# Two whole gathered columns per step fetched row by row, and running maxima stored eight columns at a time, in a three-layer graph network

## The chip, the core and the metric

The kernel runs on one core of one Trainium2 chip. The core has five engines with a queue of instructions each: TensorE (PE), VectorE (DVE), ScalarE (ACT), GpSimd (POOL) and SyncE (SP). Sixteen DMA engines serve them. The metric is the device time of one execution in microseconds (us); less is better.

## What is computed

`x` has 6250 rows (nodes) of 128 features. 200,000 edges `(src, dst)` are sorted by `dst`. After a layer norm and a ReLU, three layers each take, for every node, the maximum over its incoming edges of the source node's row, and add two products:

```python
def _sage_conv(x, src, dst, Wl, bl, Wr):
    agg = jax.ops.segment_max(x[src], dst, num_segments=x.shape[0])
    agg = jnp.where(jnp.isfinite(agg), agg, 0.0)
    return agg @ Wl + bl + x @ Wr

h = jnp.maximum(_layernorm(x, axis=-1), 0.0)
h = leaky_relu(_sage_conv(h, src, dst, Wl1, bl1, Wr1), 0.01)   # 128 -> 256 features
h = leaky_relu(_sage_conv(h, src, dst, Wl2, bl2, Wr2), 0.01)   # 256 -> 256
h = leaky_relu(_sage_conv(h, src, dst, Wl3, bl3, Wr3), 0.01)   # 256 -> 128
return x + h
```

The rows gathered are 128 floats (512 B) wide in layer 1 and 256 floats (1 KB) in layers 2 and 3.

## The kernel before

**Tiling.** The sorted edges are cut into 512 runs of 391 edges. Partition p holds four runs (`CHAINS = 4`), so one *column* is 128 edges, one in each partition, and a *group* is four columns, one edge of each of the 512 runs. Each layer walks 1564 columns in 28 steps: 27 steps of 56 columns (`STEPS - 1`, `RING_COLS`) and a last one of 52. The buffer `ring` in SBUF holds one step: 7 blocks of 8 columns, 14 groups.

**Gathers.** POOL fetches a column with one indirect DMA (L448): 128 rows of the feature table into 128 partitions. Its order of work is a plain loop over blocks and columns. Before block b of the next step it waits until DVE has scanned that block and SP has stored it (`logged[b]`).

**Rows fetched one by one.** 160 rows of every step but the last don't come through POOL: the 128 rows of column 55 and the last 32 of column 54. POOL gathers only 96 rows of column 54. SP issues 72 of these rows, 8 at a time (`fetch_rows` at L1215, nine times a step, each behind a store), and ACT issues 88, 11 at a time (`fetch_rows` at L1140, eight times in a row). Each time the engine first reads 8 or 11 row addresses from the SBUF tile `row_at` into registers (a TENSOR_LOAD, put down to L321, inside `row_places`), then issues one DMA of one row for each (L1231, L1155). A step's rows can be asked for only when block 6 of the step before has been stored (`logged[BLOCKS - 1]`); ACT also waits until DVE has used the first group of its own step (`group_scanned`).

**Scan.** For each group g, DVE adds a restart mask to the running maximum of group g-1 (L758), waits for the data of group g, and takes the maximum in place (L792). At an even g it waits for a block's gathers, at g = 13 (`GROUPS - 1`, columns 52 to 55) for the rows of SP and ACT (L785 to L790). When the first add of block b+1 is through, it stages the indices of block b (L739), which also tells POOL and SP that block b is scanned.

**Log.** SP stores every group to a log in HBM, two stores per block: the first four columns (L1240) when `group_scanned` says so, the last four (L1246) when `block_scanned` does. At the end of a layer the rows that end a node's edges are gathered from this log (L475) and projected.

**ACT's other work.** In the first 25 steps of a layer ACT also moves two tiles through PE for the `x @ Wr` part (`keep_pair`: L1104, L1109, L1118, in layer 1 also L1125 to L1131). It stands in program order behind the step's rows and ahead of the next step's.

Of the kernel before, what the change touches and what calls it, by code (L numbers as in the profile page):

```python
# [11 lines left out]
U32 = mybir.dt.uint32  # L12
U8 = mybir.dt.uint8

P = 128
BLOCKS = 7
# [15 lines left out]
SYNC_ROWS, SYNC_AT_ONCE = 72, 8  # L32
ACT_AT_ONCE = 11
ROWS = 160
# [8 lines left out]
def gnn_program(nc, x, src, dst, weights, out, nodes):  # L43
# [40 lines left out]

    ROWS_OF = [(0, SYNC_ROWS), (SYNC_ROWS, ROWS - SYNC_ROWS)]
    FETCHED = [DMA * count for _, count in ROWS_OF]
    assert LAST <= RING_COLS - CHAINS and all(f * (STEPS - 1) < 1 << 16 for f in FETCHED)
    assert SYNC_ROWS % SYNC_AT_ONCE == 0 and (ROWS - SYNC_ROWS) % ACT_AT_ONCE == 0
    assert SYNC_ROWS // SYNC_AT_ONCE <= GROUPS - 3

    def by_pool(b, last):

        return width(b, last) - (b == BLOCKS - 1 and not last)
# [3 lines left out]
    STORES_OF = [width(b, False) // CHAINS for b in range(BLOCKS)]  # L97
# [7 lines left out]
    with ExitStack() as ctx:  # L105
# [173 lines left out]
        LOADS = 8  # L279
# [29 lines left out]
        def list_of(edges_src):  # L309

            pairs = []
            for first, count, run in ((0, P, (CHAINS - 1) * P), (P, ROWS - P, (CHAINS - 1) * P - (ROWS - P))):
                chain = run * RUN + GROUPS - 1
                pairs.append((row_list[:, first:first + count],
                              bass.AP(edges_src.tensor, chain, [[GROUPS, STEPS - 1], [RUN, count]])))
            return pairs
# [25 lines left out]
        def _(pool):  # L342
# [48 lines left out]
            with pool.If(pool.value_load(unsorted[0:1, 0:1], min_val=0, max_val=1 << 24)):  # L391
# [23 lines left out]
                pool.wait_ge(list_loaded, 2 * DMA)  # L415
                with nc.allow_non_contiguous_dma(reason="one word of each row to fetch"):
                    for here, there in list_of(sorted_src):
                        pool.dma_start(here, there).then_inc(sort_done, DMA)
                pool.wait_ge(sort_done, DMA * (3 + LOADS))

            for l, (w, _n) in enumerate(shapes):
# [12 lines left out]
                def gather(i, first, last):  # L434
                    for b in used_blocks(last):
# [9 lines left out]
                        for u in range(by_pool(b, last)):  # L445
                            c = b * BLOCK_COLS + u
                            rows = 2 * P - ROWS if c == RING_COLS - 2 and not last else P
                            pool.indirect_dma_start(  # L448
                                ring[0:rows, c * w:(c + 1) * w], None, tables[l],
                                bass.IndirectOffsetOnAxis(  # L450
                                    ap=stage[0:rows, b, u:u + 1].bitcast(U32), axis=0),
                            ).then_inc(late_landed if last and b == LATE_BLOCK and u >= CHAINS else landed[b], DMA)
# [29 lines left out]
        def _(dve):  # L482
# [207 lines left out]
            dve.wait_ge(list_loaded, 2 * DMA)  # L690
# [488 lines left out]
        def _(sp):  # L1179
# [27 lines left out]
            with nc.allow_non_contiguous_dma(reason="one word of each row to fetch"):  # L1207
                for here, there in list_of(src):
                    sp.dma_start(here, there).then_inc(list_loaded, DMA)
# [3 lines left out]
            for l, (w, n) in enumerate(shapes):  # L1213

                def fetch_rows(i, g):  # L1215

                    first = g * SYNC_AT_ONCE
# [11 lines left out]
                    places = row_places(0, mybir.EngineType.SP, i, first, SYNC_AT_ONCE, w)  # L1229
# [79 lines left out]
```

## Time and profile before

| what | value |
|---|---|
| median of 3 runs | 6050.79 us (6049.64 to 6051.76) |
| the profiled execution | 6050.56 us |
| its span | 6048.9 us |
| POOL busy | 4524.8 us, 75% |
| DVE busy | 2893.5 us, 48% |
| PE busy | 732.5 us, 12% |
| ACT busy | 225.4 us, 4% |
| DMA busy share | 0.36 in layer 1, 0.68 in layers 2 and 3 |

"Busy" doesn't count the issue of a DMA, register loads or waits, so an engine that only issues DMAs (SP, and ACT in its row fetches) looks idle here. What such an engine does is seen in the timeline and at the sources, where its entries are named SPq and ACTq. Layer 1 runs from 45 to about 1960 us, layer 2 from 2037 to 3962, layer 3 from 4044 to 5969.

### The profile page before, as it was taken

What the parts mean: (1) busy time and instruction counts of PE and PEld (TensorE: products, weight loads), DVE (VectorE), ACT (ScalarE), POOL (GpSimd) and SP (SyncE); (2) the same over time, 40 slices, a digit from 0 to 9 for tenths busy, and PEclk for the clock granted to TensorE, in tenths of its full rate; (3) what the DMA queues carried; (4) which work ended last, traced back from release to release, by engine and by line L of the source; (5) the groups of instructions that cost most, each with busy time, mean ns of one, the idle gap of its engine ahead of it and who ended that gap; (6) DMA issues with size and microseconds to landing.
All of it is one profiled execution on the core that took longest, in us unless ns stands there. A gap on an engine that the chain in (4) does not pass through costs nothing.

```text
span 6048.9 us, 53349 instructions
## 1 busy us (share of the span) xinstructions
PE 732.5 (12%) x2214; PEld 411.8 (7%) x2214; DVE 2893.5 (48%) x3638; ACT 225.4 (4%) x664; POOL 4524.8 (75%) x4793
## 2 busy tenths in 40 slices
PE   1111111111100311111111110040010000100003
PEld 0000000000000200000000000030000000000002
DVE  5333333333333555555555555565555555555556
ACT  1000000000000100000000000010000000000001
POOL 6777777777777777777777777767777777777776
PEclk7555555555555655555555555575555555555556
DMA  4333333333333566666666666666666666666665
GB/s 141 108 111 107 108 108 109 110 108 108 108 108 107 171 216 218 218 216 220 216 218 218 216 219 214 215 206 219 217 220 215 218 218 216 220 215 218 215 216 175
DMA packets 461123, 1089.10 MB, mean 180 GB/s; under 512 B 116295, under 2 KB 181740, under 8 KB 461068
## 3 DMA queue, kind: packets, MB, share of 16 engines
q0 software_dynamic: 203520, 519.10, 30.6%
q1 hardware_dynamic: 220508, 544.04, 24.8%
q10 hardware_dynamic: 37040, 25.45, 1.5%
q14 instruction: 48, 0.39, 0.0%
q8 instruction: 7, 0.11, 0.0%
HBM read 555.08 MB, written 533.07 MB: 180 GB/s over the span
## 4 chain that ended last, share of the span: by engine, by line
POOL 49%; issue 17%; DMA 1%; POOLq 1%; DVE 0%; PE 0%; DVEq 0%
POOL ring L448 47%; POOL ring L475 2%; POOLq L444 0%; DMA ring<-running_max_log,end_row 0%; POOLq L441 0%; DMA patch<-running_max_log,patch_row 0%; DMA ring<-features,stage 0%; DMA running_max_log<-patch 0%; POOL patch L465 0%; DVE z_sum L902 0%; DVE agg L894 0%; POOLq L455 0%; POOLq L443 0%; DMA features<-h_out 0%; DVE patch L873 0%
## 5 line engine op out<-in xcount | busy, mean ns | idle before, releaser
L448 POOL DMA_INDIRECT ring<-features,stage x4611 | 4360.0, 946 | 1432.2 <-issue 1383.7
L792 DVE TENSOR_TENSOR ring<-banks,ring 128x1024 f32<-128x1024 f32 (+1 forms) x1173 | 1227.4, 1046 | 2954.0 <-DMA ring<-features,stage 2918.9
L758 DVE TENSOR_TENSOR banks<-ring,banks 128x1024 f32<-128x1024 f32 (+1 forms) x1173 | 1232.1, 1050 | 37.5
L975 PE MATMUL banks<-wr,h_turned 128*128 128x256 f32 (+1 forms) x490 | 220.7, 596 | 3623.4 <-ACT h_turned L1109 3623.4
L975 PEld LDWEIGHTS banks<-wr,h_turned 128*128 128x128 f32 x490 | 127.2, 320 | 3687.4 <-ACT h_turned L1109 3678.6
L991 PE MATMUL banks<-dst_low,own 128*128 128x394 bf16 x200 | 100.4, 502 | 976.0 <-DVE own L734 976.0
L475 POOL DMA_INDIRECT ring<-running_max_log,end_row x147 | 142.9, 972 | 65.6 <-issue 43.9
L1109 ACT ACTIVATE h_turned<-banks 128x256 f32<-128x256 f32 (+1 forms) x147 | 51.8, 353 | 3128.6 <-issue 2664.1
L739 DVE COPY stage<-edges 128x8 int32 (+1 forms) x588 | 119.4, 203 | 88.0 <-DVE banks L758 32.8
L977 PE MATMUL banks<-b,ones 1*128 1x256 f32 (+1 forms) x294 | 157.6, 637 | 0.0
L1048 PE MATMUL banks<-wl,agg 128*128 128x256 f32 (+1 forms) x490 | 110.7, 369 | 1.2 <-DVE agg L894 0.9
L992 PE MATMUL banks<-dst_high,own 128*128 128x394 bf16 x200 | 99.1, 496 | 0.0
L991 PEld LDWEIGHTS banks<-dst_low,own 128*128 (+1 forms) x200 | 27.8, 139 | 1023.0 <-issue 1021.8
L967 PE MATMUL banks<-ident,h_in 128*128 128x128 f32 x245 | 86.6, 436 | 27.8 <-DMA h_in<-features 27.8
L1125 ACT ACTIVATE signs<-banks,node 128x391 bf16<-128x391 f32 x50 | 29.6, 592 | 1505.5 <-issue 1501.8
L1048 PEld LDWEIGHTS banks<-wl,agg 128*128 128x128 f32 x490 | 84.3, 210 | 11.1 <-DVE agg L894 4.0
L977 PEld LDWEIGHTS banks<-b,ones 1*128 1x128 f32 x294 | 72.9, 307 | 74.4 <-issue 74.4
L1175 ACT ACTIVATE agg<-zeros 128x512 f32<-128x512 f32 x75 | 47.3, 631 | 761.1 <-PE banks L1048 761.1
L1017 PE MATMUL banks<-ident,ring 128*128 128x128 f32 x20 | 5.0, 425 | 577.8 <-DVEq L804 577.8
L1036 PE MATMUL banks<-ident,ring 128*128 128x128 f32 x245 | 59.2, 319 | 62.7 <-DMA ring<-running_max_log,end_row 59.0
L1118 ACT ACTIVATE own<-banks 128x256 f32 (+3 forms) x147 | 51.1, 348 | 394.0 <-PE banks L977 394.0
L883 DVE TENSOR_SCALAR finite<-banks 128x512 int32<-128x512 int32 (+2 forms) x75 | 44.3, 591 | 42.1 <-PE banks L1036 41.2
(114 smaller groups left out, 523.4 us busy)
## 6 DMA issues: line engine op xcount, KB each, us to landing
running_max_log<-ring SPq DMA_DIRECT2D x782, 512.0 KB, 3.1
running_max_log<-ring SPq DMA_DIRECT2D x391, 256.0 KB, 2.2
ring<-features ACTq DMA_DIRECT2D x4752, 1.0 KB
ring<-features,stage POOLq DMA_INDIRECT x4611, 3.2
ring<-features SPq DMA_DIRECT2D x3888, 1.0 KB
ring<-features ACTq DMA_DIRECT2D x2376, 0.5 KB
ring<-features SPq DMA_DIRECT2D x1944, 0.5 KB
h_in<-features ACTq DMA_DIRECT2D x98, 128.0 KB, 2.5
```

The costliest lines, as they stand in the source:

```text
L448: pool.indirect_dma_start(ring[0:rows, c * w:(c + 1) * w], None, tables[l], bass.IndirectOffsetOnAxis(ap=stage[0:rows, b, u:u + 1].bitcast ...
L475: pool.indirect_dma_start(ring[:, t * w:(t + 1) * w], None, logs[w], bass.IndirectOffsetOnAxis(ap=end_row[:, t:t + 1].bitcast(U32), axis=0 ...
L739: dve.tensor_copy(stage[:, b, :], src_t[:, bass.ds((i + ahead) * RING_COLS + b * BLOCK_COLS, BLOCK_COLS)]).then_inc(block_scanned, 1)
L758: dve.tensor_tensor(sum_ps[:, 0:CHAINS * w].rearrange("p (h f) -> p h f", h=CHAINS), group(g - 1).rearrange("p (h f) -> p h f", h=CHAINS), ...
L792: dve.tensor_tensor(group(g), sum_ps[:, 0:CHAINS * w], group(g), ALU.max).then_inc(turn, 1)
L967: turn = pe.transpose(turn_ps[0][:, c * P:(c + 1) * P], h_in[p][:, c * P:(c + 1) * P], ident[:, :])
L975: pe.matmul(mm_ps[p][:, 0:n], h_turned[p][:, c, :], wr_sb[l][:, c, :], start=(c == 0), stop=False)
L977: pe.matmul(mm_ps[p][:, 0:n], ones[0:1, :], b_sb[l][:, :], start=False, stop=True).then_inc(own_mm, 1)
L991: pe.matmul(sel_ps[p][:, 0:RUN + 3], chosen, dst_low[:, h, :], start=(h == 0), stop=False)
L992: mm = pe.matmul(sel_ps[p][:, 0:RUN + 3], chosen, dst_high[:, h, :], start=False, stop=(h == CHAINS - 1))
L1036: turn = pe.transpose(turn_ps[b][:, t * w + c * P:t * w + (c + 1) * P], ring[:, k * w + c * P:k * w + (c + 1) * P], ident[:, :])
L1048: mm = pe.matmul(mm_ps[b][:, t * n:(t + 1) * n], agg[b][:, t * w + c * P:t * w + (c + 1) * P], wl_sb[l][:, c, :], start=(c == 0), stop=(c ...
```

## The change

- Rows fetched one by one are now exactly two columns, 54 and 55 (`FETCHED_COLS = 2`): 256 rows a step. SP fetches the 128 of column 55, ACT the 128 of column 54. POOL issues 54 gathers a step and none of fewer than 128 rows.
- SP reads 16 addresses at a time and issues 16 rows, eight times a step: two such groups behind each of the stores of blocks 0 to 3. ACT reads 32 addresses at a time and issues 32 rows, four times.
- In all steps but the last SP stores a block with one store of eight columns, after the whole block is scanned. The last step keeps its stores of four columns.

```diff
-SYNC_ROWS, SYNC_AT_ONCE = 72, 8
-ACT_AT_ONCE = 11
-ROWS = 160
+FETCHED_COLS = 2
+SYNC_ROWS = 128
+AT_ONCE, ACT_AT_ONCE = 16, 32
...
     def by_pool(b, last):
 
-        return width(b, last) - (b == BLOCKS - 1 and not last)
+        return width(b, last) - (FETCHED_COLS if b == BLOCKS - 1 and not last else 0)
...
-    STORES_OF = [width(b, False) // CHAINS for b in range(BLOCKS)]
+    STORES_OF = [1 for b in range(BLOCKS)]
...
-            before, p = divmod(ROWS_OF[k][0] + r, P)
-            c = RING_COLS - 1 - before
-            p += before * (2 * P - ROWS)
+            ahead, p = divmod(ROWS_OF[k][0] + r, P)
+            c = RING_COLS - 1 - ahead
...
-                            rows = 2 * P - ROWS if c == RING_COLS - 2 and not last else P
                             pool.indirect_dma_start(
-                                ring[0:rows, c * w:(c + 1) * w], None, tables[l],
+                                ring[:, c * w:(c + 1) * w], None, tables[l],
...
-                        if columns > CHAINS:
+                        if last and columns > CHAINS:
                             sp.wait_ge(group_scanned, i * BLOCKS + (FIRSTS * l + b + 1))
                             sp.dma_start(log_block(l, i, b, 0, CHAINS), ring[:, c * w:(c + CHAINS) * w]
                                          ).then_inc(logged[b], DMA)
-                            if not last and BLOCK_GROUPS * b * SYNC_AT_ONCE < SYNC_ROWS:
-                                fetch_rows(i, BLOCK_GROUPS * b)
                         sp.wait_ge(block_scanned, i * BLOCKS + (SIGNED * l + BLOCKS + b + 1))
-                        at = columns - CHAINS
-                        sp.dma_start(log_block(l, i, b, at, CHAINS), ring[:, (c + at) * w:(c + columns) * w]
+                        at = columns - CHAINS if last else 0
+                        sp.dma_start(log_block(l, i, b, at, columns - at), ring[:, (c + at) * w:(c + columns) * w]
                                      ).then_inc(logged[b], DMA)
-                        if not last and (BLOCK_GROUPS * b + 1) * SYNC_AT_ONCE < SYNC_ROWS:
-                            fetch_rows(i, BLOCK_GROUPS * b + 1)
+                        for g in (BLOCK_GROUPS * b, BLOCK_GROUPS * b + 1):
+                            if not last and g * AT_ONCE < SYNC_ROWS:
+                                fetch_rows(i, g)
```

The waits for the loaded lists (`list_loaded`, `LOADS`) follow the number of columns; the two lists are now two columns of `row_list`.

SP, the start of the loop over layer 2's steps, before. ISA and REGISTER_ALU are waits and register work, `ring` 128x1024 is a group of four columns.

```order
L1240 ISA
L1240 DMA running_max_log<-ring 128x1024
L1228 ISA
L321 ISA
L321 TENSOR_LOAD row_at
L1231 DMA ring<-features 1x1024 x8
L1244 REGISTER_ALU
L1246 ISA
L1246 DMA running_max_log<-ring 128x1024
L321 REGISTER_ALU
```

The same place now; `ring` 128x2048 is a block of eight columns.

```order
L1240 ISA
L1240 DMA running_max_log<-ring 128x2048
L1224 ISA
L319 ISA
L319 TENSOR_LOAD row_at
L1227 DMA ring<-features 1x1024 x16
L319 REGISTER_ALU
L319 TENSOR_LOAD row_at
L1227 DMA ring<-features 1x1024 x16
L1238 REGISTER_ALU
```

Between two stores SP now has 32 rows and two loads of 16 registers, where it had 8 rows and one load of 8; the first store of a step waits for the whole block 0.

ACT, the start of a step behind the tiles' part (layer 1's last loop), before.

```order
L1169 ISA
L1151 REGISTER_ALU
L321 ISA
L321 TENSOR_LOAD row_at
L1155 DMA ring<-features 1x512 x11
L321 REGISTER_ALU
```

The same place now.

```order
L1165 ISA
L1147 REGISTER_ALU
L319 ISA
L319 TENSOR_LOAD row_at
L1151 DMA ring<-features 1x512 x32
L319 REGISTER_ALU
```

From the load on, the pattern stands eight times with 11 rows before and four times with 32 rows now. On POOL the loop body loses one gather: `128x256 x6` and `96x256` at its end become `128x256 x6`.

## Rows read from the trace of the kernel before

**Rows 1.** The page: the chain that ended last, shares by engine.
```profile
POOL 49%; issue 17%; DMA 1%; POOLq 1%; DVE 0%; PE 0%; DVEq 0%
```

**Rows 2.** Windows in layers 2 and 1: length, POOL busy (instructions), clock, DMA share, GB/s.
```profile
2600.00:2668.75 68.75, 51.98 (x56) 0.50 0.68 217
1000.00:1068.75 68.75, 51.97 (x56) 0.52 0.36 109
```

**Rows 3.** Timeline of POOL: start, duration, what; the first is the 96-row gather.
```profile
1064.98 0.91 POOL L448 DMA_INDIRECT ring<-features,stage  x1 [0.30 <-issue]
1066.20 0.95 POOL L448 DMA_INDIRECT ring<-features,stage  x1 [0.30 <-issue]
```

**Rows 4.** Timeline of ACT, layer 2: a step's 88 rows, end of the tiles behind.
```profile
3016.72 54.39 ACTq L1155 DMA_DIRECT2D ring<-features  x88
...
3079.33 0.38 ACT L1118 ACTIVATE own<-banks 128x256 f32 x1 [3.40 <-PE banks L977]
```

**Rows 5.** ACT's address loads in layer 2 (ns, start): its first; a step's first, fifth.
```profile
L321 ACTq TENSOR_LOAD <-row_at x1: 2628/2628/2628, 2050.1 to 2050.1; - x1
...
L321 ACTq TENSOR_LOAD <-row_at x1: 2586/2586/2586, 3014.0 to 3014.0; - x1
...
L321 ACTq TENSOR_LOAD <-row_at x1: 1442/1442/1442, 3042.9 to 3042.9; - x1
```

**Rows 6.** All address loads of layer 1, then of layer 2: ns min/median/max.
```profile
L321 SPq TENSOR_LOAD <-row_at x240: 969/1096/1337, 61.0 to 1875.5; - x120
L321 ACTq TENSOR_LOAD <-row_at x214: 1421/2701/3389, 59.4 to 1879.4; - x107
...
L321 SPq TENSOR_LOAD <-row_at x241: 692/1397/1947, 2061.3 to 3879.9; - x121
L321 ACTq TENSOR_LOAD <-row_at x215: 1423/3014/4004, 2057.4 to 3890.0; - x108
```

**Rows 7.** Timeline of ACT's last 18 rows in a step; DVE's maximum behind them.
```profile
2647.94 10.52 ACTq L1155 DMA_DIRECT2D ring<-features  x18
...
2660.71 1.23 DVE L792 TENSOR_TENSOR ring<-banks,ring 128x1024 f32<-128x1024 f32 x1 [0.23 <-DVEq L790]
```

**Rows 8.** Timeline of DVE, layer 2, from a step's last maximum on.
```profile
3005.18 1.23 DVE L792 TENSOR_TENSOR ring<-banks,ring 128x1024 f32<-128x1024 f32 x1
...
3007.82 0.17 DVE L739 COPY stage<-edges 128x8 int32 x1 [0.16 <-DVE banks L758]
3012.57 1.22 DVE L792 TENSOR_TENSOR ring<-banks,ring 128x1024 f32<-128x1024 f32 x1 [4.57 <-DMA ring<-features,stage]
...
3017.74 0.17 DVE L739 COPY stage<-edges 128x8 int32 x1 [0.16 <-DVE banks L758]
```

**Rows 9.** Timeline of SP, layer 2: block 6's second store, then 8 rows.
```profile
3008.16 0.33 SPq L1246 DMA_DIRECT2D running_max_log<-ring  x1
...
3021.25 2.52 SPq L1231 DMA_DIRECT2D ring<-features  x8
```

**Rows 10.** Page: SP's stores in layers 2 and 3, then 1; last number: us to landing.
```profile
running_max_log<-ring SPq DMA_DIRECT2D x782, 512.0 KB, 3.1
running_max_log<-ring SPq DMA_DIRECT2D x391, 256.0 KB, 2.2
```

**Rows 11.** Waits of DVE for single rows: us in total, times, longest.
```profile
DVE ring L792 <- DVEq L790: 15.1, 12, 4.6
```

**Rows 12.** POOL's load of the unsorted flag, one register (ns).
```profile
L391 POOLq TENSOR_LOAD <-unsorted x1: 1167/1167/1167, 27.2 to 27.2; - x1
```

**Rows 13.** Timeline of ACT, layer 1: a step's rows, end of the tiles behind.
```profile
1011.42 49.28 ACTq L1155 DMA_DIRECT2D ring<-features  x88
...
1069.37 0.38 ACT L1118 ACTIVATE own<-banks 128x256 f32 x1 [2.55 <-PE banks L977]
```

**Rows 14.** Timeline of layer 2's end: POOL's last gather, DVE's last maximum.
```profile
3957.34 0.95 POOL L448 DMA_INDIRECT ring<-features,stage  x1 [0.30 <-issue]
...
3960.59 1.21 DVE L792 TENSOR_TENSOR ring<-banks,ring 128x1024 f32<-128x1024 f32 x1
```

More of the change, by code:

```diff
@@ L87, in gnn_program @@
     assert LAST <= RING_COLS - CHAINS and all(f * (STEPS - 1) < 1 << 16 for f in FETCHED)
-    assert SYNC_ROWS % SYNC_AT_ONCE == 0 and (ROWS - SYNC_ROWS) % ACT_AT_ONCE == 0
-    assert SYNC_ROWS // SYNC_AT_ONCE <= GROUPS - 3
+    assert SYNC_ROWS % AT_ONCE == 0 and (ROWS - SYNC_ROWS) % ACT_AT_ONCE == 0
+    assert SYNC_ROWS // AT_ONCE <= GROUPS - 3
     def by_pool(b, last):
-        return width(b, last) - (b == BLOCKS - 1 and not last)
+        return width(b, last) - (FETCHED_COLS if b == BLOCKS - 1 and not last else 0)
     OPENING = [CHAINS if b == LATE_BLOCK else width(b, True) for b in range(BLOCKS)]
     LANDED = [DMA * ((STEPS - 1) * by_pool(b, False) + OPENING[b]) for b in range(BLOCKS)]
-    STORES_OF = [width(b, False) // CHAINS for b in range(BLOCKS)]
+    STORES_OF = [1 for b in range(BLOCKS)]
     LOGGED = [DMA * ((STEPS - 1) * STORES_OF[b] + width(b, True) // CHAINS) for b in range(BLOCKS)]
@@ L278, in gnn_program @@
         LAYERS = len(shapes)
-        LOADS = 8
+        LOADS = 6 + FETCHED_COLS
         CONSTS = 16 + 2 * CHAINS
@@ L307, in run_neighbours, with lists_of @@
             return pairs
[L309 to L316, printed above, removed]
+        def lists_of(edges_src):
+            return [(row_list[:, k * P:(k + 1) * P],
+                     bass.AP(edges_src.tensor, (CHAINS - 1 - k) * P * RUN + GROUPS - 1, [[GROUPS, STEPS - 1], [RUN, P]]))
+                    for k in range(FETCHED_COLS)]
         def row_places(k, engine, i, at, count, w):
@@ L414, in _ @@
                         pool.dma_start(dest, there).then_inc(sort_done, DMA)
-                pool.wait_ge(list_loaded, 2 * DMA)
+                pool.wait_ge(list_loaded, FETCHED_COLS * DMA)
                 with nc.allow_non_contiguous_dma(reason="one word of each row to fetch"):
-                    for here, there in list_of(sorted_src):
+                    for here, there in lists_of(sorted_src):
                         pool.dma_start(here, there).then_inc(sort_done, DMA)
@@ L446, in gather @@
                             c = b * BLOCK_COLS + u
-                            rows = 2 * P - ROWS if c == RING_COLS - 2 and not last else P
                             pool.indirect_dma_start(
-                                ring[0:rows, c * w:(c + 1) * w], None, tables[l],
+                                ring[:, c * w:(c + 1) * w], None, tables[l],
                                 bass.IndirectOffsetOnAxis(
-                                    ap=stage[0:rows, b, u:u + 1].bitcast(U32), axis=0),
+                                    ap=stage[:, b, u:u + 1].bitcast(U32), axis=0),
                             ).then_inc(late_landed if last and b == LATE_BLOCK and u >= CHAINS else landed[b], DMA)
@@ L689, in _ @@
             dve.memset(restart_turns[:, :, 0], LOWEST).then_inc(prep_done, 1)
-            dve.wait_ge(list_loaded, 2 * DMA)
+            dve.wait_ge(list_loaded, FETCHED_COLS * DMA)
             for w in widths:
@@ L1207, in _ @@
             with nc.allow_non_contiguous_dma(reason="one word of each row to fetch"):
-                for here, there in list_of(src):
+                for here, there in lists_of(src):
                     sp.dma_start(here, there).then_inc(list_loaded, DMA)
@@ L1215, in fetch_rows @@
                 def fetch_rows(i, g):
-                    first = g * SYNC_AT_ONCE
+                    first = g * AT_ONCE
                     if g == 0:
@@ L1228, in fetch_rows @@
                             sp.wait_ge(logged[BLOCKS - 1], i * (DMA * STORES_OF[BLOCKS - 1]) + LOGGED[BLOCKS - 1] * l)
-                    places = row_places(0, mybir.EngineType.SP, i, first, SYNC_AT_ONCE, w)
+                    places = row_places(0, mybir.EngineType.SP, i, first, AT_ONCE, w)
                     for r, place in enumerate(places):
```

1 line of the change is left out of this document (added).

## The prediction

> **What bounds the kernel now.** I read the chain that ended last first: half of the span is POOL itself and 17% more is POOL's issue between two gathers [rows 1]. The windows then show a step: 68.75 us in layer 1 and in layer 2 alike, though the DMA share is 0.36 in one and 0.68 in the other [rows 2]. POOL's timeline explains it: gather after gather, 1.25 us from start to start with 0.30 us between them, never a wait; 55 x 1.25 = 68.75 [rows 3]. So POOL's count of gathers sets a step, and neither bytes nor DVE do.
>
> The second thing to see is who else has a full step. Busy shares hide it, since issues and register loads aren't counted. ACT's timeline in layer 2 has 88 row DMAs from 3016.72 to 3071.11 [rows 4], behind a load that began at 3014.0 [rows 5]: 57.1 us, then tiles until 3079.71, 8.6 us more. The rows of the next step can't be asked for before block 6 is free again. DVE waited for such rows 12 times already, 15.1 us in all [rows 11], at no cost, because POOL ran ahead meanwhile. The change takes work from POOL and gives 40 rows a step to ACT and 56 to SP.
>
> **POOL's part.** The gather that goes cost 1.22 us from start to start [rows 3]. 27 steps a layer: 32.9 us, three layers: 98.8 us. If nothing else becomes late, the time is 6050.6 - 98.8 = 5951.8 us.
>
> **The loop through the single rows, layer 2.** The path is: load of addresses and issue of rows, landing, DVE's last maximum, first add and staging of the next step, store of block 6, its landing, next load. Term by term:
>
> - A row on ACT. 57.1 us less eight loads of 3.01 (median [rows 6]) is 33.0 for 88 rows: 0.375 us each. 128 rows: 48.0 us.
> - Landing. ACT's last row was issued by 2658.46, the maximum that waited for it began at 2660.71 [rows 7]: 2.25 us.
> - From that maximum to the issue of the store of block 6: 3005.18 to 3008.16 [rows 8, 9], 2.98 us.
> - Landing of the store. 256 KB take 2.2 us, 512 KB 3.1 [rows 10]. A block of eight columns is 1 MB in layers 2 and 3: at 0.9 us for each 256 KB more, 4.9 us (no faster than 3.1, no slower than twice that).
>
> With L for a load of 32 addresses and 0.1 us to start again, ACT's cycle is 48.0 + 2.25 + 2.98 + 4.9 + 0.1 + 4L = 58.2 + 4L. The tiles (8.6 us) lie beside the last four terms and are hidden.
>
> SP likewise: 8 rows take 2.52 us [rows 9], 0.33 a row at the pace from start to start, 128 rows 42.2 us; three stores between its groups and small gaps 3.1 us; a load of 16 addresses eight times, 8M. After its last row: 2.25 landing, then DVE from the last maximum to the staging of block 0 (2.64 + 0.17 to the first staging, and 5.34 from the next step's first maximum to the end of the second [rows 8], 8.2 us together with the gap), because the store of block 0 now waits for the whole block and stands ahead of the first row; 0.5 for that store. 56.3 + 8M.
>
> **What a load costs** decides, and the trace has none of this size. Loads of 8 addresses on SP have a median of 1.10 us in layer 1 and 1.40 in layer 2; loads of 11 on ACT have 2.70 and 3.01 [rows 6]. But ACT's are of two kinds: the fifth of a step always takes 1.44 us [rows 5]; its addresses begin at word 116 of the row, a multiple of four, and most of the others do not (the first of a step does, at 72, and took 2.59 us there). All offsets of the changed kernel are multiples of 16 words, so I take the short kind. Through 8 words at 1.10 and 11 at 1.44 a line has 0.115 us a word. Lower bound: no growth, L = 1.44 and M = 1.40; a load of one register took 1.17 us on POOL [rows 12], so some of it is fixed. Upper bound: all words at the pace of the long kind, 2.70 / 11 = 0.245 us, L = 7.8 and M = 3.9. I take the line, which is nearest to the rows that are aligned as the new ones: L = 1.44 + 21 x 0.115 = 3.9, and M = 2.2, between the line drawn on from layer 1's 1.10 (2.0) and from layer 2's 1.40 (2.3).
>
> The Trainium skill has two rules on this, which disagree. "Runtime: NRT & Kernel Launch", section Instruction fetch mechanics, puts a register load at about 200 ns a register even in bulk (an estimate by it: L 6.4 and M 3.2, ACT's cycle 83.8 us and SP's 81.9). This case's 8 words in 1.10 us are cheaper, its 11 unaligned ones dearer. "DMA: Bandwidth & Descriptors", section Latency and other measured facts, has a floor of about 600 ns and says that unrolling by four amortizes it; a load that is mostly floor speaks against my forecast and for the first rival below. The shortest of SP's, 0.69 us, fits that floor.
>
> **Sum for layers 2 and 3.** ACT's cycle is 58.2 + 15.6 = 73.8 us, SP's 56.3 + 17.6 = 73.9, POOL's 67.5: a step takes 73.9 us. This doesn't go into the layer in full, since POOL runs ahead and the last step fetches no single rows. SP's first load comes when block 0 is staged, about 4.5 us after ACT's load of now, 2050.1 [rows 5]; 45.3 + 17.6 + 2.25 later, at about 2120, is the first step's last maximum; 26 steps later, at 2120 + 26 x 73.9 = 4041, the last fetched rows are in; 36 us of DVE (13 groups at 2.52 us and small things) end the layer's scan at 4077. Before it ended at 3960.6 [rows 14]. So a layer grows by 26T - 1804, here 117 us, and two by 235. The layer is POOL's again below T = 68.1, and the whole change breaks even at T = 70.0.
>
> **Layer 1.** ACT: 49.28 us [rows 13] less the seven loads in it at 2.70 [rows 6] is 30.4 for 88 rows, 44.2 for 128; with 15.6 for loads and 9.05 for the tiles [rows 13], which here are longer than the path through the store, 68.9 us. SP: 42.2 + 3.1 + 8 x 2.0 + 2.25 + 5 + 0.5 = 69.1, the 5 being the 8.2 with operations of half the width. By the same reckoning as above (a first step of about 68 us, 26 more, 20.5 of DVE) this layer stays POOL's up to about 68.9, so both stand at the edge. I count its full 33 us as gained.
>
> Sum: +235 - 33 = +202 on the profiled execution's 6050.6 us (which is 0.2 us from the median): 6252 us.
>
> **Edits at nothing.** One store per block instead of two takes seven issues of 0.38 us from SP and moves the same bytes; its wait for the whole block delays the first rows (in SP's sum above). The gathers' own wait for `logged[b]` has most of a step of room. Of the 256 rows, 96 more small transfers share DMA engines that are at 0.68; if they queue, landing grows, which the range holds.
>
> **The rivals.**
> - Loads hardly grow (M up to 1.5, L up to 2.4). Then ACT's cycle is at most 67.8 and SP's 68.3, POOL decides all three layers, and the time is 5952. For it: one register costs as much as eight [rows 12, 6], and ACT gets rid of four loads and of the long kind. Against it: 11 words of the short kind take a third more than 8. This ends on the other side of my forecast; it decides below T = 70.0, or M = 1.7. Chance 23%.
> - Loads go in proportion: M = 2 x 1.40 = 2.8, SP's cycle 78.7 and each of layers 2 and 3 up by 242; layer 1 at 70.6 a step up by 12. 6547 us. For it: the contention of layer 2 (1.40 against 1.10) should fall on each word. Chance 15%.
> - All words at the pace of the long kind, L = 7.8: ACT's cycle 89.4, 520 us more in each of two layers, 390 in layer 1, about 7480. For it: the first load of a step in layer 2 took 2.59 us though aligned [rows 5]. Against it: the fifth repeats at 1.44, and 8 words at 1.10 are not that dear. Chance 7%.
> - Gain and loss cancel, T between 69.8 and 70.2: 5%.
>
> **How the numbers follow.** My forecast, with L from 3.0 to 4.4 and M from 1.7 to 2.6, has 50% and steps of 70.2 to 77.1 us, so 6060 to 6430. Faster 23%, within 0.2% (about what a measurement of this kernel tells from no change) 5%, slower 72%. The range goes from 5945, which takes the first rival in, to 6500; the last two rivals lie above.
>
> **What the profile would show.** POOL's gathers should have gaps longer than 0.30 us in layers 2 and 3, ended by staging or by a store's landing, and DVE's wait for the single rows should grow from 15.1 us to hundreds. Windows of a step there should be near 73.9 us, in layer 1 near 67.5. The loads of 16 and 32 addresses are read off directly: above 1.7 and 3.0 us my forecast holds, below them it is wrong. If the row pace in groups of 32 is not 0.375 us, the first term is wrong; if the step is long but the loads are short, the landings are.

## The result, and the profile after

| | before | after |
|---|---|---|
| median | 6051.2 us (4 runs, 6049.6 to 6051.8) | 6306.7 us (4 runs, 6302.0 to 6310.2) |
| profiled execution (span) | 6050.6 (6048.9) | 6307.1 (6305.4) |
| a step, mean of steps 2 to 27, layers 1 / 2 / 3 | 68.78 / 68.74 / 68.62 | 67.80 / 74.87 / 74.94 |

The changed kernel takes 1.0422 times as long (95% interval 1.0404 to 1.0440). Means of steps are taken from DVE's last maximum of one step to that of the next.

First the length of a step: windows of POOL from one step's last maximum to the next, in layer 2 and in layer 1 (length, POOL busy with its instructions, clock, DMA share, GB/s).

```profile
3061.55:3135.77 74.22, 51.06 (x54) 0.50 0.61 202
1056.64:1123.90 67.26, 50.78 (x55) 0.53 0.37 111
```

POOL's busy time is what it was less one gather, but the window of layer 2 is 5.5 us longer than in [rows 2]. The DMA share fell from 0.68 to 0.61, so it isn't bytes either. Layer 1's window is shorter, by about the gather. The waits of DVE (us in total, times, longest) name what ends a step:

```profile
DVE ring L788 <- DVEq L786: 2063.2, 81, 38.2
DVE ring L788 <- DMA ring<-features,stage: 1145.2, 217, 14.9
```

The first row is the wait for the single rows. It was 15.1 us in 12 times [rows 11] and is 2063.2 us in 81, which is each of the 27 steps of each of three layers. POOL, which never waited [rows 3], now has a hole at the start of each step. Its timeline from the end of the step before the window, and its next hole:

```profile
3057.53 0.95 POOL L444 DMA_INDIRECT ring<-features,stage  x1 [0.30 <-issue]
3058.78 0.95 POOL L444 DMA_INDIRECT ring<-features,stage  x1 [0.30 <-issue]
3064.27 0.94 POOL L444 DMA_INDIRECT ring<-features,stage  x1 [4.54 <-issue]
3065.52 0.95 POOL L444 DMA_INDIRECT ring<-features,stage  x1 [0.31 <-issue]
...
3124.42 0.94 POOL L444 DMA_INDIRECT ring<-features,stage  x1 [2.91 <-issue]
```

The trace calls the 4.54 us "issue". Counted from the first gather of layer 2, with 54 to a step, the gather behind this hole is the first of block 4, and the one behind the 2.91 us is the first of block 3. Each has to wait for SP's store of the same block of the step before. SP issued these two stores at 3058.44, behind its last row, and at 3117.27, between two groups of rows; by the trace's semaphore records they had landed at 3063.48 and 3123.63, and each gather starts 0.79 us after that. So both holes come from SP's queue: its stores go out late because they stand behind its rows. They are not what ends a step. That is the wait for the rows, the last row of DVE's timeline from one last maximum to the next (the first staging here is block 6's, the second block 0's):

```profile
3061.55 1.22 DVE L788 TENSOR_TENSOR ring<-banks,ring 128x1024 f32<-128x1024 f32 x1 [36.81 <-DVEq L786]
3062.81 1.23 DVE L754 TENSOR_TENSOR banks<-ring,banks 128x1024 f32<-128x1024 f32 x1
3064.20 0.17 DVE L735 COPY stage<-edges 128x8 int32 x1 [0.16 <-DVE banks L754]
...
3069.57 0.17 DVE L735 COPY stage<-edges 128x8 int32 x1 [0.16 <-DVE banks L754]
...
3135.77 1.23 DVE L788 TENSOR_TENSOR ring<-banks,ring 128x1024 f32<-128x1024 f32 x1 [36.75 <-DVEq L786]
```

Which engine was late is read from the two queues. SP, then ACT, in that step (start, duration from the first to the last of the group):

```profile
3073.80 11.84 SPq L1227 DMA_DIRECT2D ring<-features  x32
3085.91 0.38 SPq L1240 DMA_DIRECT2D running_max_log<-ring  x1
3089.78 11.64 SPq L1227 DMA_DIRECT2D ring<-features  x32
...
3121.12 11.60 SPq L1227 DMA_DIRECT2D ring<-features  x32
```

```profile
3071.22 55.26 ACTq L1151 DMA_DIRECT2D ring<-features  x128
...
3134.68 0.38 ACT L1114 ACTIVATE own<-banks 128x256 f32 x1 [3.40 <-PE banks L973]
```

SP issued its last row at 3132.72 and the maximum came 3.05 us later; ACT had its last out by 3126.48, 6.2 us sooner. From the maximum at 3061.55 to SP's next load at 3070.5 are 8.95 us, from there to SP's last row 62.2, and 3.05 to the maximum: 74.2. Over the 26 steps of layer 2 the same three parts are 9.04, 62.4 and 3.39 us on average: 74.87. The loads of the same step, by engine (ns min/median/max, first and last start), SP's first and its second, and ACT's four:

```profile
L319 SPq TENSOR_LOAD <-row_at x8: 1190/2115/3300, 3070.5 to 3126.3; - x8
L319 ACTq TENSOR_LOAD <-row_at x4: 2169/2214/2222, 3069.0 to 3111.9; - x4
...
L319 SPq TENSOR_LOAD <-row_at x1: 3208/3208/3208, 3070.5 to 3070.5; - x1
L319 SPq TENSOR_LOAD <-row_at x1: 1191/1191/1191, 3079.1 to 3079.1; - x1
```

SP's eight are 3.21, 1.19, 3.30, 1.20, 3.01, 1.19, 3.28 and 1.22 us: a load right behind a store of 1 MB takes 3.2, one between two groups of rows 1.2. The stores themselves (page, KB and median us to landing; for 1 MB the median is of block 6's stores alone, the only ones whose landing the profile pairs with a wait):

```profile
running_max_log<-ring SPq DMA_DIRECT2D x378, 1024.0 KB, 4.5
running_max_log<-ring SPq DMA_DIRECT2D x215, 512.0 KB, 3.4
```

### The profile page after: what moved, and what is told of

Same layout as the page of the kernel before. It is cut to its first block and busy times, and to the rows that moved or that the text cites. A ratio compares the mean times of both kernels' runs of the same rounds, so it can differ in the third digit from the quotient of the medians.

```text
span 6305.4 us, 65820 instructions
## 1 busy us (share of the span) xinstructions
PE 729.7 (12%) x2214; PEld 411.3 (7%) x2214; DVE 2867.6 (45%) x3638; ACT 225.5 (4%) x664; POOL 4449.6 (71%) x4712
## 5 line engine op out<-in xcount | busy, mean ns | idle before, releaser
L444 POOL DMA_INDIRECT ring<-features,stage x4530 | 4283.8, 946 | 1752.4 <-issue 1726.1
L788 DVE TENSOR_TENSOR ring<-banks,ring 128x1024 f32<-128x1024 f32 (+1 forms) x1173 | 1227.7, 1047 | 3236.2 <-DVEq L786 2063.2
L1032 PE MATMUL banks<-ident,ring 128*128 128x128 f32 x245 | 58.8, 319 | 62.4 <-DMA ring<-running_max_log,end_row 61.2
```

Source lines behind the costliest of these rows:

```text
L444: pool.indirect_dma_start(ring[:, c * w:(c + 1) * w], None, tables[l], bass.IndirectOffsetOnAxis(ap=stage[:, b, u:u + 1].bitcast(U32), axi ...
L788: dve.tensor_tensor(group(g), sum_ps[:, 0:CHAINS * w], group(g), ALU.max).then_inc(turn, 1)
L1032: turn = pe.transpose(turn_ps[b][:, t * w + c * P:t * w + (c + 1) * P], ring[:, k * w + c * P:k * w + (c + 1) * P], ident[:, :])
```

## The experiments

T is a step of layer 2. Diffs are against the changed kernel unless said otherwise. "Before" in the same sessions stood at 6049.3 to 6052.7 us.

### Does each half of the loss need the other: no rows, no stores, only the stores

**No single rows.** Left out: all 256 rows a step; the ring's columns 54 and 55 keep what they held.

```diff
-                            dve.wait_ge(act_rows_landed, FETCHED[1])
...
-                            dve.wait_ge(sync_rows_landed, FETCHED[0])
...
-                    fetch_rows(j)
...
-                            if not last and g * AT_ONCE < SYNC_ROWS:
-                                fetch_rows(i, g)
```

> The changed kernel without any of the 256 single rows a step (columns 54 and 55 keep what they held) and without the waits for them. Theory A: POOL alone sets all steps at 54 x 1.25 = 67.5 us, layers 1 to 3 each 33 us shorter than before: about 5950 us. Rival: if the stores of eight columns or DVE bound as well, above 6000 us.

Measured 5949.9 us (5949.1 to 5951.2), ratio 0.9831 [0.9815, 0.9848]; T 67.5.

```profile
2600.00:2667.50 67.50, 0.00 (x0) 0.00 (x0) 34.39 (x36) 0.00 (x0) 51.06 (x55) 0.50 0.64 214
```

The row has all engines (PE, PEld, DVE, ACT, POOL). POOL's gain is 101 us, against 98.8 forecast, and the whole difference to the changed kernel, 357 us, hangs on the single rows.

**No stores** but in the last step of a layer. Left out: the stores, and the gathers that read them back read the table instead.

```diff
-                        sp.dma_start(log_block(l, i, b, at, columns - at), ring[:, (c + at) * w:(c + columns) * w]
-                                     ).then_inc(logged[b], DMA)
+                        if last:
+                            sp.dma_start(log_block(l, i, b, at, columns - at), ring[:, (c + at) * w:(c + columns) * w]
+                                         ).then_inc(logged[b], DMA)
+                        else:
+                            sp.sem_inc(logged[b], DMA)
```

> The changed kernel without its stores in all steps but the last (SP raises the semaphore instead; the gathers at a layer's end read the feature table in place of the log). Theory A (SP's loop: 128 rows, eight loads, and 2 us for each of four 1 MB stores a load stands behind): the loads take 1.2 us each, SP's loop is about 64 us, ACT's no longer, POOL sets all steps at 67.5 us: about 5950 us. Rival R (256 single rows a step are too many for what serves them, whatever else runs): step over 70 us in layers 2 and 3, time over 6050 us.

Measured 5954.3 us (5952.8 to 5954.8), ratio 0.9840 [0.9823, 0.9856]; T 67.5. The loads of two steps, SP's and ACT's:

```profile
L319 SPq TENSOR_LOAD <-row_at x18: 1161/1179/1203, 3002.5 to 3144.0; - x18
...
L319 ACTq TENSOR_LOAD <-row_at x9: 2150/2202/2253, 3004.6 to 3139.7; - x9
```

Every load of 16 addresses takes 1.18 us now and none 3.2. So 1.2 us is the price of the load, and the other 2.0 come from the store ahead of it. ACT's 128 rows took 49.87 us in place of 55.26: rows beside stores cost more too, 0.34 against 0.38 us each.

**Block stores alone**, put into the kernel before.

```diff
-    STORES_OF = [width(b, False) // CHAINS for b in range(BLOCKS)]
+    STORES_OF = [1 for b in range(BLOCKS)]
...
-                        at = columns - CHAINS
+                        at = columns - CHAINS if last else 0
```

> The kernel before, only the stores changed to one of eight columns per block; 160 rows a step as before. Theory A: POOL goes on to set the step at 68.75 us; SP has 72 rows only; ACT starts a step's rows after the landing of a 1 MB store (4.5 us in place of 3.1), 65.5 + 1.4 = 66.9 us in all, still under 68.75: 6050 us, within 0.3%. Rival S (the stores of eight columns cost by themselves): above 6100 us.

Measured 6052.1 us (6049.7 to 6052.6), ratio 1.0002 [0.9988, 1.0017]. DVE's wait for the single rows is 326.2 us in 53 times there, 15.1 before, and costs nothing, since POOL still bounds the layers. A wait's total isn't a loss.

### The other half alone: the new rows with stores of four columns

```diff
-    STORES_OF = [1 for b in range(BLOCKS)]
+    STORES_OF = [width(b, False) // CHAINS for b in range(BLOCKS)]
...
-                        if last and columns > CHAINS:
+                        if columns > CHAINS:
...
+                            if not last and BLOCK_GROUPS * b * AT_ONCE < SYNC_ROWS:
+                                fetch_rows(i, BLOCK_GROUPS * b)
```

> Two columns fetched row by row as in the changed kernel, stores of four columns as before. Theory A (SP's loop through its 128 rows sets the step, 74.9 us on average in layers 2 and 3; a load of 16 addresses takes 1.2 us alone and 3.2 us right behind a 1 MB store): all eight loads now stand behind a 512 KB store, about 2.1 us each, so 16.9 us in place of 17.6; four more stores among the rows add 2 us; the first rows come a group earlier, 2.7 us. Step 73.5 us, time about 6235 us. Rival S (the stores of eight columns, with their wait for the whole block, made the kernel slower, not the rows): about 6050 us or less.

Measured 6482.2 us (6476.4 to 6485.7), ratio 1.0707 [1.0689, 1.0725]: both theories missed, and smaller stores make it worse. SP's loads over two steps, then packets of the queue that fetches instructions, in layer 2 (2150 to 3900) and layer 3 (4250 to 5900):

```profile
L319 SPq TENSOR_LOAD <-row_at x16: 1163/2195/2387, 2999.7 to 3135.7; - x16
```

```profile
q14 instruction: 112, 0.92, 0.2%
...
q14 instruction: 13, 0.11, 0.0%
```

Seven of eight loads now stand right behind a store of 512 KB and take 2.0 to 2.3 us, about 1.0 more than alone; the first of a step takes 1.2. Seven times 1.0 is nearly what 4 x 2.0 was: dividing the stores saved 1.1 us of loads a step in layer 2 and cost seven more issues. Theory A missed mostly in the first rows. They were to come 2.7 us earlier; SP's first load comes 10.4 us after the maximum in layer 3, later than the changed kernel's 9.0, because it waits for block 6's last store, and stores land in 6.3 us there (median of the page). Layer 2 has a further 3.3 us a step (79.5 against 76.2 in layer 3), together with 112 instruction packets against 13. These 3.3 us lie between the maximum and SP's first load (13.6 against 10.4 us). The same code sits in both layers, so I put them to fetching instructions anew on each turn of the loop; no run took that fetching away alone. It agrees with the Trainium skill ("Runtime: NRT & Kernel Launch", Instruction fetch mechanics), by which most engines hold 32 KiB of instructions in two blocks and a taken branch to a target outside them forces a fetch; the page has no price for it. In the changed kernel layers 2 and 3 have 2 and 5 such packets in the same stretches: it isn't its loss.

### What a load costs

**SP reads 32 at once.**

```diff
-AT_ONCE, ACT_AT_ONCE = 16, 32
+AT_ONCE, ACT_AT_ONCE = 32, 32
...
-                        for g in (BLOCK_GROUPS * b, BLOCK_GROUPS * b + 1):
-                            if not last and g * AT_ONCE < SYNC_ROWS:
-                                fetch_rows(i, g)
+                        if not last and b * AT_ONCE < SYNC_ROWS:
+                            fetch_rows(i, b)
```

> The changed kernel, SP reads 32 addresses at a time and issues 32 rows behind each of four stores. Theory A, by ACT's loads of 32 (2.2 us against 1.2 for 16 on SP, so 0.06 us an address): four loads of about 4.2 us behind a store in place of 3.2 + 1.2 each, step shorter by about 1 us, about 6250 us. Rival F (the load's cost is fixed, addresses are free): four loads of 3.2 us, step shorter by 4.8 us, about 6070 us. Rival P (0.115 us for each address, as forecast): no change, 6300 us.

Measured 6311.8 us (6310.8 to 6313.2), ratio 1.0429 [1.0411, 1.0446]: no change against the changed kernel.

```profile
L319 SPq TENSOR_LOAD <-row_at x8: 4119/4232/4290, 3002.0 to 3122.8; - x8
```

SP's last 32 rows of a step and the maximum behind them, on the timeline:

```profile
3127.02 10.23 SPq L1227 DMA_DIRECT2D ring<-features  x32
...
3141.81 1.23 DVE L788 TENSOR_TENSOR ring<-banks,ring 128x1024 f32<-128x1024 f32 x1 [37.11 <-DVEq L786]
```

A load of 32 behind a store is 4.2 us = 2.2 + 2.0: the 2.0 are paid once per store, whatever the load's size, and four loads a step of 4.2 are 16.9 us, against the changed kernel's 17.6. The landing took 4.6 us (3137.25 to 3141.81) where it took 3.05, which gives that back. So the loads came out as in theory A and the time as in rival P.

**The kernel before, ACT reading 22 at once** (a single run).

```diff
-ACT_AT_ONCE = 11
+ACT_AT_ONCE = 22
```

> The kernel before, ACT reads 22 addresses at a time (four loads, at words 72, 94, 116 and 138 of the row; 72 and 116 are multiples of four). Theory V (a load takes 0.25 us for each access and 0.2 besides; an access brings four addresses where they are aligned, one where not; that gives 1.2 us for 16 and 2.2 for 32 aligned ones and 1.44 for 11): 1.95 us at words 72 and 116 (five fours and two ones), about 5 us at 94 and 138. Rival P (only the count matters, 0.06 us an address): all near 1.6 us. Time 6050 us by both, POOL sets the step.

Measured 6052.7 us. The four loads of one step in layer 1; they begin at words 72, 94, 116 and 138 of the list:

```profile
L321 ACTq TENSOR_LOAD <-row_at x1: 2214/2214/2214, 1010.9 to 1010.9; - x1
...
L321 ACTq TENSOR_LOAD <-row_at x1: 5418/5418/5418, 1020.6 to 1020.6; - x1
...
L321 ACTq TENSOR_LOAD <-row_at x1: 1935/1935/1935, 1033.5 to 1033.5; - x1
...
L321 ACTq TENSOR_LOAD <-row_at x1: 5484/5484/5484, 1042.9 to 1042.9; - x1
```

At 72 and 116, multiples of four, 22 addresses take about 2 us; at 94 and 138, which are none, 5.4. An estimate that fits: 0.2 us + 0.25 us per access. The addresses are counted off in fours from the load's first; four that begin at a multiple of four are one access, all others are an access each. That gives 1.95 and 5.7 us here, 1.2 for 16, 2.2 for 32, and 1.45 and 2.95 for 11. The rows are 1.94 to 2.2 and 5.4; 1.18; 2.20; 1.44 and 2.70 to 3.01 [rows 5, 6]. It holds for loads with no large store ahead: in layer 2 of this run, beside stores of 512 KB, the four loads of a step (from 3017.1 on) take 2.8, 7.1, 2.5 and 7.2 us.

### Which queue is the bound: rows moved from SP to ACT

```diff
-SYNC_ROWS = 128
-AT_ONCE, ACT_AT_ONCE = 16, 32
+SYNC_ROWS = 112
+AT_ONCE, ACT_AT_ONCE = 16, 24
```

> The changed kernel with 16 of SP's rows given to ACT: SP 112 (seven groups of 16), ACT 144 (six groups of 24). Theory A (the slower of two issue loops sets a step; SP's is 74.9 us, ACT's about 68): SP loses 16 x 0.33 + 1.2 = 6.5 us and is at 68.4; ACT gains 16 x 0.38 = 6.1 and two loads of about 1.7, less what four of 2.2 were over six of 1.7, 7.5 in all: 75.5 us. Time about 6320 us, and DVE then waits for ACT. Rival E (the DMA engine behind all single rows is full; who issues them doesn't matter): no change, 6300 us, with SP or ACT done many us before DVE goes on.

Measured 6745.5 us (6744.6 to 6751.0), ratio 1.1151 [1.1135, 1.1167]; T 81.0. SP's last rows of a step, ACT's 144 and DVE's maximum, then ACT's loads over the stretch:

```profile
3086.89 5.08 SPq L1227 DMA_DIRECT2D ring<-features  x16
...
3040.62 66.88 ACTq L1151 DMA_DIRECT2D ring<-features  x144
...
3109.24 1.22 DVE L788 TENSOR_TENSOR ring<-banks,ring 128x1024 f32<-128x1024 f32 x1 [44.21 <-DVEq L786]
```

```profile
L319 ACTq TENSOR_LOAD <-row_at x7: 1714/1747/6283, 3037.5 to 3119.4; - x7
```

SP was done at 3091.97 and DVE waited for ACT's last row of 3107.50: the bound went over to ACT, as expected, but a step takes 5.5 us more than the 75.5 expected. One of ACT's loads takes 6.28 us where its like take 1.75. It is the last of the step, and it begins as SP, now out of rows, issues two stores of 1 MB right behind each other:

```profile
3092.23 1.02 SPq L1240 DMA_DIRECT2D running_max_log<-ring  x2
...
L319 ACTq TENSOR_LOAD <-row_at x1: 6283/6283/6283, 3092.9 to 3092.9; - x1
```

Two stores at 2.0 us each on top of 1.75 make 5.75. The median of this last load over the steps of layer 2 is 5.9 us, and ACT's six loads sum to 14.9 us a step on average, 4.4 more than six of 1.75. Layer 2 has 109 instruction packets again (386 in the whole run, 184 in the changed kernel), but none falls into this load: the nearest are at 3077.4 and 3107.6. So the stores are most of the 5.5 us. ACT's first load comes 9.6 us after the maximum, 1.8 later than in the changed kernel; for that part the fetch stays possible.

### Can the loss be taken off: loads ahead of the stores

**Loads ahead.** SP reads the addresses of the next 16 rows before it waits for the block and stores it.

```diff
+                        fetching = not last and BLOCK_GROUPS * b * AT_ONCE < SYNC_ROWS
+                        if fetching:
+                            places = places_of(i, BLOCK_GROUPS * b)
...
+                        if fetching:
+                            issue_rows(i, BLOCK_GROUPS * b, places)
+                            issue_rows(i, BLOCK_GROUPS * b + 1, places_of(i, BLOCK_GROUPS * b + 1))
```

> The changed kernel, but SP reads the addresses of the first group of each block ahead of that block's store instead of behind it. Theory A (the 2 us are the load's, for reading behind a store that is being handed to the DMA engines): 4 x 2 us go, and block 0's load is hidden in the wait for the block: SP's loop 65.7 us, so ACT's loop or POOL sets the step, about 68 us, time 5960 to 5990 us, under both kernels. Rival Q (the queue is busy behind a store, whatever comes next): the first row behind each store waits the 2 us instead, only 1.2 us a step are saved, about 6245 us.

Measured 6328.0 us (6325.1 to 6339.3), ratio 1.0454 [1.0436, 1.0471]; T 75.6, steps alternating near 78 and 73. My theory, that this would give 5960 to 5990, fell. Loads of SP in a step of 73.0 us and ACT's in the step before, then SP's rows and the maximum of the first:

```profile
L319 SPq TENSOR_LOAD <-row_at x8: 1189/1204/2989, 3077.0 to 3132.3; - x8
...
L319 ACTq TENSOR_LOAD <-row_at x4: 4280/4314/4339, 3003.4 to 3048.9; - x4
```

```profile
3081.96 13.11 SPq L1235 DMA_DIRECT2D ring<-features  x32
...
3126.77 11.90 SPq L1235 DMA_DIRECT2D ring<-features  x32
...
3146.09 1.22 DVE L788 TENSOR_TENSOR ring<-banks,ring 128x1024 f32<-128x1024 f32 x1 [35.56 <-DVEq L786]
```

The loads did shrink, to 11.4 us a step from 17.6. But 32 rows behind a store took 11.9 to 13.1 us where they had taken 11.6 to 11.8 (+3.8 a step), and the maximum came 7.4 us after the last row, out by 3138.67, and not 3.05. ACT's loads of 32 took 4.3 us, not 2.2, when a store of SP's had gone out just before (at 3003.26 for the first). This makes the steps alternate: in the one of 78.2 us all four of ACT's loads stand 0.2 to 0.6 us behind a store of SP's, 8.2 us more in all than in the next step, and its last row is the last to land; in the one of 73.0 us they take 2.2 to 2.4 and SP's is. So the 2.0 us aren't tied to SP's queue: register loads on either engine pay them, and with SP's loads out of the way its rows and their landing got longer.

**Are the bytes of the rows the cause?** Rows of 64 bytes in place of 1 KB (left out: the rest of each row), first alone, then with the loads ahead.

```diff
-            return tables[l].rearrange("n f -> (n f)").bitcast(U8)[bass.ds(place, 4 * w)].rearrange("(a b) -> a b", a=1)
+            return tables[l].rearrange("n f -> (n f)").bitcast(U8)[bass.ds(place, 64)].rearrange("(a b) -> a b", a=1)
```

> The changed kernel, each single row's DMA moves 64 bytes in place of 512 or 1024 (columns 54 and 55 get only 16 floats). Same issues, same loads. Theory A (issue loop): landing of the last row falls from 3 us to about 2, time 6250 to 6300 us. Rival E (the rows' DMA engine is full): a row costs it far less, time under 6100 us.

> The kernel with the addresses loaded ahead of the stores, whose last rows landed 7.4 to 11.4 us after their issue (6328 us), with single rows of 64 bytes (columns 54 and 55 get only 16 floats). Theory E (there the rows pile up in front of their DMA engine): the landing falls to 2 to 3 us and the step by 5 to 8 us, to about 68 us, time about 5990 us. Rival Q (issue is what is slow, whatever the bytes): above 6250 us.

Measured 6281.2 us (6277.8 to 6282.2), ratio 1.0381 [1.0366, 1.0396], T 74.4; and 6302.6 us (6300.5 to 6304.8), ratio 1.0417 [1.0403, 1.0432]. A sixteenth of the bytes takes 0.4% off. With the loads ahead the landing still is 5.1 us (SP's last row 3129.15, maximum 3134.23). So the bytes of the rows are not the cause.

**Loads ahead, and no rows on ACT** (left out: column 54's 128 rows). To the edit of the loads ahead comes:

```diff
-                            dve.wait_ge(act_rows_landed, FETCHED[1])
-                            dve.sem_inc(act_rows_landed, -FETCHED[1])
...
-                    fetch_rows(j)
```

> The kernel with the addresses loaded ahead of the stores (6328 us, step 75.5 us), without ACT's 128 single rows (column 54 keeps what it held); SP as it was. Theory G (SP's and ACT's DMAs are prepared by one thing that both share, so what is saved on one side comes back as late landing): without ACT's rows SP's last row lands 2 to 3 us after its issue in place of 7, and SP's rows behind a store keep their full pace: step 68 us, about 5985 us. Rival O (SP's own stores delay SP's rows): step stays over 73 us, over 6200 us.

Measured 6019.1 us (6018.8 to 6020.8), ratio 0.9948 [0.9931, 0.9964]; T 69.7.

```profile
3114.44 12.91 SPq L1227 DMA_DIRECT2D ring<-features  x32
...
3129.12 1.23 DVE L786 TENSOR_TENSOR ring<-banks,ring 128x1024 f32<-128x1024 f32 x1 [31.80 <-DVEq L784]
```

The maximum came 1.8 us after the last row, out by 3127.35. So the long landings come from SP's and ACT's rows being under way together. Theory G was right on the landing and wrong on the pace, where rival O was. SP's own pace behind a store, 12.9 us for 32 rows, is the same without ACT: that part is between a store and the rows of one queue.

**Rows first**: 32 of SP's rows go ahead of block 0's store, and block 6 is stored in halves, the second right behind the last maximum.

```diff
+                    if not last:
...
+                        fetch_rows(i, 0)
...
+                        if split:
+                            sp.wait_ge(step_scanned, i + (STEPS * l + 2))
...
+                        if not last and (b + 1) * AT_ONCE < SYNC_ROWS:
+                            fetch_rows(i, b + 1)
```

> The changed kernel with SP's loop rearranged: 32 addresses at a time; the first 32 rows of a step ahead of the store of block 0, the other three groups behind the stores of blocks 0 to 2; block 6 stored in two halves, the second as soon as the step's last maximum is there, without waiting for the first add of the next step. By the parts measured: loads 2.2 + 3 x 4.2 = 14.8, rows 42.2, three stores 1.5, landing 4.2, from the last maximum to the store's issue 1.6, landing of 512 KB 3.4, start 0.2: SP's loop 67.9 us, ACT's about 65. Step about 68 us in layers 2 and 3, time 5955 to 5990 us, faster than both kernels. Rival G (what SP issues faster comes back as late landing, as where the addresses were loaded ahead): landing 7 to 8 us, step over 71, time over 6080 us. Rival I (SP's longer loop body makes it fetch instructions in each step, 3 us a step): about 6100 us, with over 100 instruction packets in a layer.

Measured 6383.7 us (6382.4 to 6385.9), ratio 1.0548 [1.0534, 1.0563]; T 76.4, worse by 1.5 us a step than the changed kernel. SP's timeline at a step's end; its first load after it; SP's waits for that landing; the 1 MB stores on the page:

```profile
3070.07 2.25 SPq L1251 DMA_DIRECT2D running_max_log<-ring  x3
3072.58 1.06 SPq L1244 DMA_DIRECT2D running_max_log<-ring  x1
3077.11 0.33 SPq L1251 DMA_DIRECT2D running_max_log<-ring  x1
```

```profile
L320 SPq TENSOR_LOAD <-row_at x1: 2079/2079/2079, 3087.2 to 3087.2; - x1
```

```profile
SPq L320 <- DMA running_max_log<-ring: 420.0, 53, 10.9
```

```profile
running_max_log<-ring SPq DMA_DIRECT2D x324, 1024.0 KB, 6.8
```

Half of block 6 is issued at 3077.11 and its landing is seen at 3087.2, 10.1 us later: ahead of it stand three stores of 1 MB that SP couldn't issue while it was busy with rows. My premise, a small store that lands in about 3.4 us, was wrong. Rival G's long landing is there as well (the maximum 6.1 us after the last row, on average in layer 2); rival I's fetching isn't (2 and 7 packets in the stretches of layers 2 and 3). No version I ran beats the kernel before with all of its work.

## Why the prediction came out as it did

The time was forecast at 6252 and is 6307, the sign and the mechanism are right: rows through SP bind layers 2 and 3, POOL's gain shows only in layer 1. That the sum came so near is in part luck, by the price of a load below.

- **POOL's part**: 98.8 us forecast, 101 measured without the rows. Right.
- **Layer 1**: -33 forecast, its last maximum came at 1923.7 in place of 1957.6, -33.9. Right. SP did stand at the edge, as I had reserved: its loop took 67.8 us a step there (69.1 forecast), and POOL's without the rows 67.5. ACT (68.9 forecast) didn't: its last row was out 8.1 us before the maximum, on average, SP's 1.6.
- **Layers 2 and 3**: +117 each forecast; measured from first gather to last maximum 1923.3 to 2065.9 and 1923.4 to 2071.8, so +143 and +148. The rule 26T - 1804 holds with T = 74.9: it gives 143. The first step (82.4 us in layer 2, 82.7 forecast) and the last (36.8, 36) fit. Of the miss of 55 us, 52 are one microsecond in T, in 52 steps; 4 more are layer 3's first step, 86.5 us.
- **The terms of T on SP**: on average in layer 2, last maximum to load 9.04 (8.7 forecast), load to last row 62.4 (62.9), landing 3.39 (2.25). The mis-sized term is the landing, by 1.1 us. I read it where ACT issued the last of its 88 rows with SP's 72 long out; now 128 stand beside 128. That this is the reason fits the run without ACT's rows, where the landing is 1.5 us on average.
- **The price of a load: right sum, wrong reason.** I forecast 8 x 2.2 = 17.6 us for SP and measured 17.6 in the step shown, which is luck. But nothing costs 0.115 us an address: 16 addresses are 1.2 us alone, and four of the eight have 2.0 us of a 1 MB store ahead of them. The stores of 1 MB, which I had put at nothing, are in this price with 2.0 us each; left as halves they would have cost nearly as much (the run with stores of four columns). On ACT the same line gave 3.9 for 32 addresses, where they take 2.2, so by my formula ACT's cycle is some 67 us and not 73.8. In the trace it is about 70.5 us, mostly since its last row lands 5.1 us after its issue (semaphore records, average of layer 2) and not 2.25. That it would stand level with SP was wrong, and my forecast's bound of "above 3.0 us" for a load of 32 failed. The line was drawn through 8 addresses behind a store of 256 or 512 KB and 11 with three accesses of one word, two different prices. The first load of a step in [rows 5], 2.59 us though aligned, was the sign of it that I passed over. It began at 3014.04, and beside it stands:

```profile
3014.05 0.33 SPq L1240 DMA_DIRECT2D running_max_log<-ring  x1
```

  That is a store of 512 KB, and 1.44 + 1.0 is near the 2.59.
- **Register loads by the Trainium skill.** The Trainium skill's some 200 ns a register ("Runtime: NRT & Kernel Launch", Instruction fetch mechanics), which it gives for the loads that the runtime adds to a program, doesn't hold for these loads from SBUF: 32 took 2.2 us, 0.07 each; where each address is an access of its own, 22 took 5.4, 0.25 each, and there it is near. The Trainium skill's floor of about 600 ns for such a load ("DMA: Bandwidth & Descriptors", Latency and other measured facts) is near the 0.69 of the shortest load [rows 6]; the cost grows with accesses from there.
- **The first rival** (loads hardly grow, 5952) had ACT's side right, L = 2.2. It failed on SP, M being 2.2, for the reason of the stores. Without stores it would have been the outcome: 5954.3 us.
- **The rivals above**: proportional loads (6547) and the long kind (7480) both fell, M 2.2 and L 2.2.
- **What the profile would show**: DVE's wait of hundreds of us came as 2063. The row pace of ACT is (55.26 - 3 x 2.2) / 128 = 0.38 us, 0.375 forecast. POOL's gaps are there; the trace names them "issue", and the count of gathers and the semaphore records put them to landings of stores, one of the two that I had named.

Open: what it is in the path of a load or a row that a 1 MB store holds up, and why the landing grows by 4 us and more when SP's loads are moved ahead. The runs show where, not in which part of the chip.

## What to carry to other kernels

An engine that only issues DMAs can be full while its busy share reads zero: add up its issues, its address loads and its waits for landings over a step before work is moved to it, and look for the smallest slack over all engines, not for the relief of the busiest. In these runs a large store delayed what was asked for right behind it (address loads on SP and on ACT, rows on SP), by 1.0 us at 512 KB and 2.0 at 1 MB for a load; dividing it or moving the loads ahead of it moved the delay and didn't remove it. A price fitted through two points holds only if both are of one kind: look for the kinds (aligned or not, behind a store or not) in single rows before a line is drawn through medians.

## What the runs showed of the hardware

- A load of n addresses from SBUF into registers, with no large store ahead of it (an estimate from the values behind): 0.2 us + 0.25 us per access, where four addresses, counted from the load's first, are one access if they begin at a multiple of four, and every other address is one. 16 addresses 1.18 us, 32 2.20, 22 from a multiple of four 1.94 to 2.2, 22 from elsewhere 5.4.
- Behind a store of 512 KB it took 1.0 us more (2.2 for 16), behind 1 MB 2.0 more (3.2 for 16, 4.2 for 32 on SP; 4.3 for 32 on ACT, behind a store that SP had issued). Behind two of 1 MB ACT's load of 24 took 6.28, against 1.75.
- A single row costs its issuer 0.33 us on SP and 0.34 to 0.38 on ACT whether it has 64 bytes or 1 KB; right behind a 1 MB store, with the loads moved ahead, 0.37 on SP.
- A store of 1 MB lands in 4.5 us (median of block 6's in the changed kernel, and of all in the run without rows), and in 6.8 where rows go ahead of the stores and three of these go out together; 512 KB behind them took 10.1.
- The maximum came 3.4 us after SP's last row where 128 rows of ACT's were under way too, and 1.5 without them (averages of layer 2; the latter with the loads ahead).
